# Four chained attention blocks on one core: row fills copied by VectorE, positions moved, and the DMAs of the transposed maxima issued by GpSimd

## The chip, the cores and the metric

The kernel runs on one core of a Trainium2 chip. A core has TensorE (PE: matmuls and transposes, results in PSUM), VectorE (DVE), ScalarE (ACT), GpSimd (POOL) and SyncE (SP). SP only issues DMAs here; DMAs can also be issued by ACT and POOL. The engines run side by side, each through its own program in order, and wait for each other by semaphores. The metric is the device time of one execution in microseconds (us); lower is better.

## The reference

Sixteen batches of 128 tokens with 128 channels go through four blocks. `ctx` is a second input of the same shape.

```python
# L0: 8 heads of 16
h = layernorm(x);  c = layernorm(ctx)
x = x + softmax(q(h) @ k(c).T / 4) @ v(c)
# L1: 16 heads of 8, causal and key padding mask, query padding
x = x + where(query_ok, softmax(where(mask, q(x) @ k(ctx).T / 8**.5, -inf)), 0) @ v(ctx)
# L2: 16 heads, then a gelu network of width 512
x = x + attn(x, ctx) @ Wo + bo;  x = x + gelu_tanh(x @ W1 + b1) @ W2 + b2
# L3: self attention (causal, padding), cross attention, gelu network; a layernorm behind each
x = ln(x + selfattn(x) @ Wo1 + bo1)
x = ln(x + crossattn(x, ctx) @ Wo2 + bo2)
x = ln(x + gelu(x @ W1 + bf1) @ W2 + bf2)
```

All is float32. The maximum of each row of scores is taken off before the exponential.

## The kernel before

Two batches make a pair; eight pairs go through five parts (L0, L1, L2, L3S for the self attention, L3C for the cross attention and the rest), which gives 40 **units**, numbered u = 8 * part + pair. A unit is 128 partitions by 256 tokens, and its two batches are b = 0 and 1. Within a batch heads go in groups of four (two groups in L0, four in the others).

Scores are computed in bfloat16 with float32 accuracy. Queries and keys are split into three bfloat16 terms (ACT makes the first in "split"; POOL the others in "rest", "term1" and "term2", lines 525, 527 and 533), and six DMAs ("stack", line 432) lay products of terms row above row in a tile `pairs`, so that one matmul of 52 (L0: 96) rows gives the scores of one head. Under these rows lie four mask rows (parts L1 and up) and three rows that carry the negated row maximum.

Each group of scores is computed twice. First "score" (line 861): the result goes to DVE, which takes the maximum of each row (`max_words`, line 754). When a batch's groups are done DVE makes three terms of the maxima ("nmax", lines 764 and 767), PE transposes them ("n_tr", line 926), DVE copies the result to `max_rows` (line 770), and a DMA of 6 or 12 KB (line 448) puts them into the three rows of `pairs`. Then "attn" (line 947) computes the transposed scores with the maximum already taken off, ACT takes the exponential (`probs`, line 651), and "pv" (line 974) multiplies by the values. The first attn group of a batch waits for that batch's DMA of maxima (semaphore `max_landed`). From L1 on each attn group is interleaved with the score group of the next unit with the same b and number.

The order of all work is a table written out by hand. Every step has a position relative to eight times its unit's number (`PREPARE`, `STACK_AT`, `SCORE_AT`, `CHAIN` and so on), `schedule()` sorts the steps, and each engine runs its share of this one list in that order. A unit thus takes eight positions; its preparation begins up to 41 positions before its own attention, and the chain behind it ("a_tr", "wo", "x_tr", "w1", "w2", "out", "store") ends up to 47 positions after. The list sets no time: an engine that waits for one step holds all steps behind it.

Four engines matter for the change. SP issues, in list order, the loads of tokens (line 367), the six stack DMAs of each unit, the mask rows (line 424), the weights (line 395) and the DMAs of maxima (line 448), each behind a semaphore wait. Before the first stack DMA it issues four DMAs (line 380) that write the mask rows' query side and rows of ones for L1 to L3 into `pairs16`; their source is `constant_rows`. POOL computes the terms, the layer norms' reciprocal roots (`var_eps` and `rstd`, lines 517 and 520), the squares of the gelu (line 538), the mask rows and the last scaling (lines 545 and 549). DVE also does the layer norm's statistics and normalisation in L0 (`stats`, `normed_in`, lines 688 to 707). ACT issues four small DMAs of ones for L0 (line 558).

## Time and profile before

| | |
|---|---|
| median of three runs | 515.94 us (515.82 to 528.79) |
| the profiled execution | 511.9 us, its span 510.2 us |
| busy over the span | PE 89%, DVE 77%, ACT 64%, POOL 42% |
| mean granted TensorE clock | 0.948 of full speed |
| chain of waits, by engine | PE 64%, DVE 15%, DMA 7%, ACT 4%, SP's queue 4%, POOL 2% |
| maxima in the chain of waits (line 448's DMAs) | 5.4% of the span |

The span is the profiled part of one execution; the execution's own time is 1.7 us more. Busy shares are means over stages that differ: L0 runs from 34.6 us (the first attn group) to about 109 us, L1 to 191, L2 to 285, L3S to 382, L3C to the end, of which the last 33 us hold no attention any more but the chains of the last three units. A busy PE is not PE at its peak, since matmul ends are modelled.

### The profile page before, as it was taken

How to read it: one execution, taken by the hardware profiler on the slowest of the kernel's cores; microseconds unless marked ns; L12 is line 12 of the kernel's file. 1: busy time of each engine (PE TensorE's matmuls, PEld its weight loads, DVE VectorE, ACT ScalarE, POOL GpSimd, SP SyncE). 2: the span in 40 equal slices, each digit the busy share in tenths (PEclk: the TensorE clock that was granted, in tenths of full speed). 3: DMA queues.
4: the chain of work that ended last, by engine and by line, in shares of the span. 5: the costliest groups of instructions: out<-in, count | busy, mean ns of one | idle time of the engine just before them, and what ended most of it. 6: DMA issues, size and time to landing. Idle time of an engine off the chain costs nothing.

```text
span 510.2 us, 17171 instructions
## 1 busy us (share of the span) xinstructions
PE 455.2 (89%) x6720; PEld 306.4 (60%) x6720; DVE 391.7 (77%) x1093; ACT 325.2 (64%) x660; POOL 216.4 (42%) x256
## 2 busy tenths in 40 slices
PE   3578998799998897999999999999999899998873
PEld 2466666466665565666666666666666556665552
DVE  6669887488787776789887777888889977886362
ACT  2436666347765676677777677576777687777541
POOL 3745388465442234244444344333436434222153
PEclk9667899799999998899999999999999999999798
DMA  5634444445454443232232322223343322200000
GB/s 130 142 88 108 120 104 100 90 108 137 111 121 101 100 94 89 65 81 74 64 75 63 69 66 64 67 66 71 73 91 88 86 66 65 46 14 26 10 16 26
DMA packets 72750, 40.45 MB, mean 79 GB/s; under 512 B 7100, under 2 KB 71900, under 8 KB 72672
## 3 DMA queue, kind: packets, MB, share of 16 engines
q1 hardware_dynamic: 72564, 39.26, 33.0%
q8 instruction: 55, 0.90, 0.7%
q14 instruction: 23, 0.19, 0.1%
q10 hardware_dynamic: 108, 0.10, 0.1%
HBM read 4.74 MB, written 1.05 MB: 11 GB/s over the span
## 4 chain that ended last, share of the span: by engine, by line
PE 64%; DVE 15%; DMA 7%; ACT 4%; issue 4%; SPq 4%; POOL 2%; POOLq 0%; DVEq 0%; ACTq 0%
PE attn_ps L947 13%; PE o_ps L974 12%; PE misc_ps L1004 6%; DMA pairs<-max_rows 5%; DVE max_words L754 5%; PE misc_ps L995 4%; PE misc_ps L981 4%; PE misc_ps L909 4%; PE score_ps L828 3%; PE misc_ps L910 3%; DVE normed_in L707 3%; PE misc_ps L915 2%; SPq L432 2%; PE misc_ps L987 2%; PE misc_ps L926 2%
## 5 line engine op out<-in xcount | busy, mean ns | idle before, releaser
L754 DVE TENSOR_REDUCE max_words<-score_ps 128x4 f32<-128x512 f32 x288 | 194.6, 683 | 50.8 <-PE score_ps L861 47.5
L651 ACT ACTIVATE probs<-attn_ps 128x512 f32<-128x512 f32 x288 | 169.5, 599 | 86.9 <-PE attn_ps L947 80.3
L947 PE MATMUL attn_ps<-pairs 55*128 55x128 bf16 (+1 forms) x1152 | 115.5, 223 | 18.4 <-DMA pairs<-max_rows 10.6
L861 PE MATMUL score_ps<-pairs 52*128 52x128 bf16 (+1 forms) x1152 | 115.4, 223 | 0.5 <-DMA pairs<-terms 0.4
L525 POOL TENSOR_TENSOR rest<-qk_f,terms 128x512 f32<-128x512 f32 x40 | 46.5, 1162 | 147.1 <-ACT terms L602 147.1
L947 PEld LDWEIGHTS attn_ps<-pairs 55*128 55x128 bf16 (+1 forms) x1152 | 66.0, 96 | 63.6 <-issue 28.9
L974 PE MATMUL o_ps<-probs,v 128*32 128x128 f32 x2304 | 98.8, 285 | 0.1
L861 PEld LDWEIGHTS score_ps<-pairs 52*128 52x128 bf16 (+1 forms) x1152 | 68.6, 97 | 3.5 <-DMA pairs<-terms 1.0
L974 PEld LDWEIGHTS o_ps<-probs,v 128*32 128x32 f32 x2304 | 54.3, 110 | 23.6 <-issue 10.6
L533 POOL TENSOR_TENSOR terms<-rest,terms 128x512 bf16<-128x512 f32 x40 | 46.3, 1158 | 14.6 <-DVE max_words L767 12.2
L527 POOL TENSOR_TENSOR terms<-qk_f,terms 128x512 bf16<-128x512 f32 x40 | 46.3, 1158 | 0.0
L660 ACT ACTIVATE o_sb<-o_ps 128x256 f32<-128x256 f32 x80 | 30.8, 385 | 23.2 <-PE o_ps L974 22.8
L517 POOL TENSOR_SCALAR var_eps<-mean_var 128x2 f32<-128x2 f32 (+1 forms) x32 | 7.1, 223 | 79.6 <-DVE mean_var L692 79.4
L981 PE MATMUL misc_ps<-ident,o_sb 128*128 128x128 f32 x160 | 35.7, 306 | 0.1
L1004 PE MATMUL misc_ps<-hidden,w 128*128 128x256 f32 x128 | 33.6, 399 | 2.4 <-ACT hidden L639 2.4
L796 DVE SCALAR_TENSOR_TENSOR xT<-misc_ps,col,xT 128x256 f32<-128x256 f32 x40 | 19.2, 482 | 19.6 <-PE misc_ps L1004 14.0
L995 PE MATMUL misc_ps<-xT,w 128*128 128x256 f32 x128 | 30.9, 384 | 0.1
L1004 PEld LDWEIGHTS misc_ps<-hidden,w 128*128 128x128 f32 x128 | 23.5, 194 | 8.1 <-ACT hidden L639 2.8
L538 POOL TENSOR_TENSOR gelu_arg<-half_h 128x512 f32<-128x512 f32 x16 | 16.3, 1039 | 27.9 <-ACT half_h L636 27.9
L520 POOL TENSOR_TENSOR rstd<-var_eps,minus_half 128x2 f32<-128x2 f32 (+1 forms) x32 | 25.4, 794 | 2.7
L590 ACT ACTIVATE qk_f<-misc_ps,col 128x256 f32<-128x256 f32 x24 | 11.4, 474 | 22.7 <-PE misc_ps L910 21.3
L602 ACT ACTIVATE terms<-qk_f 128x512 bf16<-128x512 f32 x40 | 25.1, 629 | 0.6
(108 smaller groups left out, 741.7 us busy)
## 6 DMA issues: line engine op xcount, KB each, us to landing
pairs<-terms SPq DMA_DIRECT2D x240, 128.0 KB
w<-in_weights_dram SPq DMA_DIRECT2D x5, 320.0 KB, 4.8
x_tok<-in_x_dram SPq DMA_DIRECT2D x8, 128.0 KB, 2.4
c_tok<-in_ctx_dram SPq DMA_DIRECT2D x8, 128.0 KB, 2.5
pairs<-max_rows SPq DMA_DIRECT2D x64, 12.0 KB
out_dram<-x_tok SPq DMA_DIRECT2D x8, 128.0 KB, 1.8
w<-in_weights_dram SPq DMA_DIRECT2D x3, 192.0 KB, 2.5
pairs<-constant_rows SPq DMA_DIRECT2D x4, 112.0 KB
```

The costliest lines, as they stand in the source:

```text
L525: pool.tensor_tensor(rest[:, :, :], qk_f32[:, :, :], terms[:, :, 0, :], ALU.subtract)
L527: pool.tensor_tensor(terms[:, :, 1, :], qk_f32[:, :, :], terms[:, :, 0, :], ALU.subtract)\
L533: pool.tensor_tensor(terms[:, :, 2, :], rest[:, :, :], terms[:, :, 1, :], ALU.subtract)\
L651: act.activation(probs[n % PROBS_RING][:, :, :].rearrange("p h q -> p (h q)"), attn_ps[n % 2][:, :], ACT.Exp, scale=float(D // HEADS[part] ...
L660: act.activation(o_sb[n % 2][:, :], o_ps[:, 0:2 * P], ACT.Copy)\
L754: dve.tensor_reduce(max_words[ub(step) % 2][:, QUAD * g:QUAD * (g + 1)], score_ps[n % 2][:, :].rearrange("p (h k) -> p h k", h=QUAD), AX_X ...
L861: return pe.matmul(score_ps[NUM[step] % 2][:, j * S:(j + 1) * S], tile[score_rows(u), QUAD * g + j, 0, b * S:(b + 1) * S], tile[score_rows ...
L947: last = pe.matmul(attn_ps[n % 2][:, j * S:(j + 1) * S], pairs[attn_rows(u), h, 1, b * S:(b + 1) * S], pairs[attn_rows(u), h, 0, b * S:(b ...
L974: last = pe.matmul(o_ps[32 * j:32 * j + 32, region * P:(region + 1) * P], values, probs[n % PROBS_RING][:, j, :], start=part == L0 or g % ...
L981: last = pe.transpose(bank[:, k * P:(k + 1) * P], o_sb[ub(step) % 2][:, k * P:(k + 1) * P], ident[:, :])
L995: last = pe.matmul(bank[:, half * TOK:(half + 1) * TOK], weight(f"w1_{part}_{2 * b + half}"), xT[s][:, :], start=True, stop=True)
L1004: last = pe.matmul(bank[:, 0:TOK], weight(f"w2_{part}_{c}"), hidden[:, c, :], start=(c == 0), stop=(c == 3))
```

## The change

Seven things change.

1. The four DMAs of `constant_rows` into `pairs16` go. POOL builds a `template` of 128 partitions and DVE copies its rows, 32 partitions by 4096 float32 words, four times (`fill_rows`, line 384). Two copies stand behind the first `ln_norm`, one each behind the second and third. DVE's two zero fills of `v16` move to the end of L0's preparation.
2. All token loads are issued first, before any stack DMA.
3. The mask rows of L1's first four units are issued at four steps of L0's later units, not with the stack DMAs.
4. Weights come in smaller pieces in the order of use, and L2, L3S and L3C each wait for their own.
5. Every DMA of maxima is issued by POOL, at the same step "n_tr" of the list as before by SP. POOL first waits for DVE's copy.
6. Many positions move. Units 0 and 2 are prepared three and one positions earlier (`LAG`).
7. The chains of units 36 to 39 have positions of their own (`LAST`), which interleave them.

```diff
--- before.py
+++ after.py
-W_NAMES = ([f"{m}{p}" for p in range(PARTS) for m in "qkv"] + ["o2", "o3", "o4"]
-           + [f"w1_{l}_{c}" for l in (2, 4) for c in range(4)] + [f"w2_{l}_{c}" for l in (2, 4) for c in range(4)])
+W_NAMES = ([f"{m}{p}" for p in (0, 1) for m in "qkv"]
+           + [f"{m}2" for m in "qkvo"] + [f"{m}_2_{c}" for m in ("w1", "w2") for c in range(4)]
+           + [f"{m}{p}" for p in (3, 4) for m in "qkvo"] + [f"{m}_4_{c}" for m in ("w1", "w2") for c in range(4)])
 W_AT = {n: i for i, n in enumerate(W_NAMES)}
 W_FIRST = 3
-W_SECOND = 6
-W_SOME = 5
-W_PIECES = -(-(len(W_NAMES) - W_SECOND) // W_SOME)
+W_SECOND, W_THIRD, W_FOURTH = W_AT["q2"], W_AT["q3"], W_AT["q4"]
+W_EACH = {L1: 3, L2: 2}
+W_PIECES = {L2: (W_THIRD - W_SECOND) // W_EACH[L1], L3S: (W_FOURTH - W_THIRD) // W_EACH[L2],
+            L3C: (len(W_NAMES) - W_FOURTH) // W_EACH[L2]}
...
 PREPARE = {
-    L0: (("load", -41), ("ln_in", -34), ("raw_tr", -29), ("ln_norm", -31), ("ln_tr", -26),
-          ("qk", -24), ("split", -23), ("rest", -18), ("term1", -18), ("term2", -18), ("v", -20),
-          ("mask", 24)),
+    L0: (("ln_in", -34), ("raw_tr", -29), ("ln_norm", -31), ("ln_tr", -26), ("qk", -24),
+          ("split", -23), ("rest", -20), ("term1", -18), ("term2", -18), ("v", -19), ("mask", 24)),
     L1: (("qk", -26), ("split", -25), ("rest", -22), ("term1", -20), ("term2", -18), ("v", -13)),
-    L2: (("qk", -26), ("split", -25), ("rest", -24), ("term1", -21), ("term2", -21), ("v", -13)),
-    L3S: (("qk", -26), ("split", -25), ("rest", -23), ("term1", -21), ("term2", -21), ("v", -14)),
-    L3C: (("qk", -26), ("split", -25), ("rest", -25), ("term1", -25), ("term2", -21), ("v", -13)),
+    L2: (("qk", -27), ("split", -25), ("rest", -25), ("term1", -25), ("term2", -24), ("v", -15)),
+    L3S: (("qk", -26), ("split", -25), ("rest", -25), ("term1", -22), ("term2", -21), ("v", -14)),
+    L3C: (("qk", -26), ("split", -25), ("rest", -25), ("term1", -22), ("term2", -22), ("v", -13)),
 }
-STACK_AT = {L0: -17, L1: -19, L2: -22, L3S: -22, L3C: -22}
+STACK_AT = {L0: -17, L1: -19, L2: -20, L3S: -24, L3C: -18}
...
+LAG = {0: -3, 2: -1}
+LAST = {
+    36: (("a_tr", 13), ("wo", 15), ("x_tr", 19), ("x_stats", 21), ("x_norm", 23), ("x_back", 26),
+          ("w1", 27), ("w1", 27), ("w2_first", 29), ("w2", 29), ("x_tr", 34), ("x_stats", 38),
+          ("x_norm", 43), ("out", 43), ("store", 47)),
...
+            put(pos + LAG.get(u, 0), Step(kind, u, 0, 0))
...
+        for kind, pos in LAST.get(u, CHAIN[part]):
...
+        def fill_rows(dve, r):
+
+            if r == 0:
+                dve.wait_ge(rows_ready, 5)
+            rows_ = slice(HALF * (r % 2) + QUARTER, HALF * (r % 2 + 1))
+            dve.tensor_copy(pairs16[r // 2][rows_, :, :, :].rearrange("p h a n -> p h (a n)").bitcast(F32),
+                            template[rows_, :, :, :].rearrange("p a b n -> p (a b n)").bitcast(F32).unsqueeze(1)
+                            .to_broadcast([HALF - QUARTER, 16, TOK])).then_inc(fill16_done, 1)
+
...
+            for s in range(SETS):
+                first = s * PAIR
+                sp.dma_start(x_tok[s][:, :, :], x[first:first + PAIR].rearrange("b t d -> t b d"))\
+                    .then_inc(tokens_landed[s], 16)
+                sp.dma_start(c_tok[s][:, :, :], ctx_in[first:first + PAIR].rearrange("b t d -> t b d"))\
+                    .then_inc(tokens_landed[s], 16)
+                if s == 0:
...
-                if step.kind == "load" and u == 2:
-
-                    sp.wait_ge(rows_ready, 4)
-                    for r in range(RING):
-                        tile, base = pairs16[r // 2], HALF * (r % 2) + product_rows(SETS)
-                        sp.dma_start(tile[base:base + MASK_ROWS + TERMS, :, :, :].rearrange("p h a n -> p h (a n)"),
-                                     constant_rows[:, :, :, :].rearrange("p a b n -> p (a b n)").unsqueeze(1)
-                                     .to_broadcast([MASK_ROWS + TERMS, 16, 2 * TOK])).then_inc(fill16_landed, 16)
...
+                if step == the("attn", u) and part == L0 and u >= RING:
+
+                    r = u % RING
+                    sp.wait_ge(fill16_done, r + 1)
+                    sp.wait_ge(mask_l1_ready, r + 1)
+                    mask_rows(sp, SETS + r)
...
-                if step.kind == "n_tr":
-
-                    evacuated(sp, step)
-                    n = ub(step)
-                    if n == 0:
-                        sp.wait_ge(fill8_landed, 16 * RING)
-                    tile, base = stack_of(u)
-                    last_row = attn_rows(u).stop
-                    sp.dma_start(tile[last_row - TERMS:last_row, :, 0, step.b * S:(step.b + 1) * S],
-                                 max_rows[n % 4][0:TERMS * heads, :]).then_inc(max_landed[n % 4], 16)
...
+            pool.memset(template[:, :, :, :], 1.0).then_inc(ones_ready, 1)
...
+                if step.kind == "n_tr":
+
+                    evacuated(pool, step)
+                    n = ub(step)
+                    if n == 0:
+                        pool.wait_ge(fill8_landed, 16 * RING)
+                    tile, base = stack_of(u)
+                    last_row = attn_rows(u).stop
+                    pool.dma_start(tile[last_row - TERMS:last_row, :, 0, step.b * S:(step.b + 1) * S],
+                                 max_rows[n % 4][0:TERMS * HEADS[u // SETS], :]).then_inc(max_landed[n % 4], 16)
...
                 if kind == "ln_norm" and u == 0:
-
-                    for ring in range(RING // 2, RING):
-                        dve.memset(v16[ring][:, :, :], 0.0).then_inc(v_zeroed, 1)
+                    fill_rows(dve, 0)
+                    fill_rows(dve, 1)
+                if kind == "ln_norm" and u == 1:
+                    fill_rows(dve, 2)
+                if kind == "ln_norm" and u == 2:
+                    fill_rows(dve, 3)
+                if kind == "ln_norm" and u >= SETS - 2:
+
+                    ring = u % RING
+                    dve.memset(v16[ring][:, :, :], 0.0).then_inc(v_zeroed, 1)
...
-                    if u == L2 * SETS:
-                        pe.wait_ge(weights_landed, 16 * W_PIECES)
+                    if part >= L2 and s == 0:
+                        pe.wait_ge(weights_landed[part], 16 * W_PIECES[part])
```

On DVE at the start of its program the four copies stand where the two zero fills (MEMSET of v_2 and v_3) stood. Before, from the first unit's normalisation on:

```order
10 L707 TENSOR_SCALAR normed_in<-x_tok,mean_var,rstd 128x128 x2
11 L707 TENSOR_SCALAR normed_in<-c_tok,mean_var,rstd 128x128 x2
12 L714 MEMSET v_2 128x1056
13 L714 MEMSET v_3 128x1056
...
18 L698 TENSOR_SCALAR half_m<-col 128x4
19 L688 BN_STATS stats<-x_tok 128x6 x2
```

The same place in the changed kernel:

```order
11 L749 TENSOR_SCALAR normed_in<-c_tok,mean_var,rstd 128x128 x2
12 L384 COPY pairs_0<-template 32x4096 x2
13 L740 TENSOR_SCALAR half_m<-col 128x4
14 L730 BN_STATS stats<-x_tok 128x6 x2
...
18 L749 TENSOR_SCALAR normed_in<-c_tok,mean_var,rstd 128x128 x2
19 L384 COPY pairs_1<-template 32x4096
20 L798 TENSOR_TENSOR v_0<-misc_ps,row 128x8x16 x2
```

Two copies now stand ahead of the second unit's statistics, and one behind its normalisation (the fourth stands behind the third unit's).

On POOL in L2, before: the three operations that make a unit's terms, then the two squares of the gelu.

```order
130 L525 TENSOR_TENSOR rest<-qk_f,terms 128x512
131 L527 TENSOR_TENSOR terms<-qk_f,terms 128x2x256
132 L533 TENSOR_TENSOR terms<-rest,terms 128x2x256
133 L538 TENSOR_TENSOR gelu_arg<-half_h 128x512 x2
```

And in the changed kernel:

```order
165 L557 TENSOR_TENSOR rest<-qk_f,terms 128x512
166 L559 TENSOR_TENSOR terms<-qk_f,terms 128x2x256
167 L565 TENSOR_TENSOR terms<-rest,terms 128x2x256
168 L575 DMA pairs_1<-max_rows 3x16x128
169 L580 TENSOR_TENSOR gelu_arg<-half_h 128x512 x2
170 L575 DMA pairs_0<-max_rows 3x16x128
```

Each of a unit's two DMAs of maxima stands behind work of other units on POOL.

On PE at the very end, before, from the network's second product of unit 37 on (L1004 is "w2", L1010 "x_tr", L995 "w1", L1016 "x_back"):

```order
2912 L1004 MATMUL misc_ps<-hidden,w 128x256 x2
2913 L1016 MATMUL misc_ps<-ident,normed 128x128 x2
2914 L1010 MATMUL misc_ps<-ident,xT 128x128 x4
2915 L995 MATMUL misc_ps<-xT,w 128x256 x4
2916 L1004 MATMUL misc_ps<-hidden,w 128x256 x4
2917 L1016 MATMUL misc_ps<-ident,normed 128x128 x2
2918 L1010 MATMUL misc_ps<-ident,xT 128x128 x2
2919 L995 MATMUL misc_ps<-xT,w 128x256 x4
```

And in the changed kernel, where the same steps are L1054, L1060, L1045 and L1066:

```order
2919 L1054 MATMUL misc_ps<-hidden,w 128x256 x2
2920 L1060 MATMUL misc_ps<-ident,xT 128x128 x2
2921 L1045 MATMUL misc_ps<-xT,w 128x256 x4
2922 L1060 MATMUL misc_ps<-ident,xT 128x128 x2
2923 L1054 MATMUL misc_ps<-hidden,w 128x256 x2
2924 L1066 MATMUL misc_ps<-ident,normed 128x128 x2
2925 L1054 MATMUL misc_ps<-hidden,w 128x256 x2
2926 L1045 MATMUL misc_ps<-xT,w 128x256 x4
```

A transpose of another unit now stands between "w1" and "w2" of a unit, and "w1" of unit 39 directly behind "w2" of unit 38.

## Rows read from the trace of the kernel before

**Rows 1.** Busy time by stretch: length, each engine's busy us (instructions), clock, DMA share, GB/s.

```profile
34.50:109.20 74.70, 66.42 (x712) 45.87 (x714) 57.91 (x176) 41.12 (x90) 43.12 (x50) 0.87 0.45 108
109.20:190.80 81.60, 77.32 (x1620) 49.62 (x1616) 63.99 (x172) 54.08 (x105) 33.51 (x35) 1.00 0.48 109
...
285.40:382.30 96.90, 96.40 (x1716) 63.16 (x1714) 77.69 (x207) 66.85 (x133) 37.15 (x40) 1.00 0.31 71
...
477.00:510.20 33.20, 21.72 (x125) 16.00 (x124) 13.69 (x49) 10.49 (x24) 11.44 (x20) 0.86 0.06 16
```

**Rows 2.** Who waited for whom: us in total, times, longest.

```profile
PE attn_ps L947 <- DMA pairs<-max_rows: 10.6, 7, 3.5
...
PE attn_ps L828 <- DMA pairs<-max_rows: 1.9, 4, 1.4
...
PE misc_ps L909 <- DMA w<-in_weights_dram: 1.4, 1, 1.4
```

**Rows 3.** Chain of waits: start, us, from issue to landing.

```profile
32.54 1.98 DMA pairs<-max_rows
...
88.97 4.75 DMA pairs<-max_rows
...
130.44 3.48 DMA pairs<-max_rows
```

**Rows 4.** Issues of the DMA of maxima on SP: ns least, median, most.

```profile
L448 SPq DMA_DIRECT2D pairs<-max_rows x80: 698/757/782, 32.5 to 467.4; - x80
```

**Rows 5.** Groups by shape: count, busy us, mean ns, idle before, releaser.

```profile
L668 DVE MEMSET v<- 128x1056 f32 x2 | 1.9, 938 | 0.3 <-issue 0.3
...
L525 POOL TENSOR_TENSOR rest<-qk_f,terms 128x512 f32<-128x512 f32 x40 | 46.5, 1162 | 147.1 <-ACT terms L602 147.1
...
L520 POOL TENSOR_TENSOR rstd<-var_eps,minus_half 128x4 f32<-128x4 f32 x8 | 8.3, 1040 | 0.7
...
L479 POOL TENSOR_SCALAR mask_rows_l<-valid_raw 4x256 bf16<-4x256 uint8 x8 | 8.5, 1061 | 0.7
```

**Rows 6.** Timeline of the start, DVE and POOL: start, us.

```profile
19.13 1.55 DVE L707 TENSOR_SCALAR normed_in<-x_tok,mean_var,rstd 128x128 f32<-128x128 f32 x2 [3.13 <-POOL rstd L520]
20.60 2.42 DVE L707 TENSOR_SCALAR normed_in<-c_tok,mean_var,rstd 128x128 f32<-128x128 f32 x2
...
19.45 1.15 POOL L525 TENSOR_TENSOR rest<-qk_f,terms 128x512 f32<-128x512 f32 x1 [0.35 <-ACT terms L602]
```

**Rows 7.** Timeline: copies of maxima and the attn groups that need them.

```profile
69.62 0.20 DVE L770 COPY max_rows<-misc_ps 24x128 bf16<-24x128 bf16 x1
...
72.40 0.40 PE L947 MATMUL attn_ps<-pairs 99*128 99x128 bf16 x4
...
220.81 0.20 DVE L770 COPY max_rows<-misc_ps 48x128 bf16<-48x128 bf16 x1
...
223.69 0.23 PE L947 MATMUL attn_ps<-pairs 55*128 55x128 bf16 x1
```

**Rows 8.** Timeline in L2 around one copy of maxima.

```profile
215.32 0.20 DVE L770 COPY max_rows<-misc_ps 48x128 bf16<-48x128 bf16 x1
...
216.21 1.16 POOL L533 TENSOR_TENSOR terms<-rest,terms 128x512 bf16<-128x512 f32 x1
...
218.83 0.23 PE L947 MATMUL attn_ps<-pairs 55*128 55x128 bf16 x1
```

**Rows 9.** Timeline of PE at the end, its waits in brackets.

```profile
474.86 0.60 PE L947 MATMUL attn_ps<-pairs 55*128 55x128 bf16 x4 [2.06 <-ACT probs L651]
...
494.23 1.97 PE L1004 MATMUL misc_ps<-hidden,w 128*128 128x256 f32 x8 [1.02 <-ACT hidden L639]
...
496.87 0.41 PE L1010 MATMUL misc_ps<-ident,xT 128*128 128x128 f32 x2 [0.45 <-DVE xT L796]
...
500.30 1.97 PE L1004 MATMUL misc_ps<-hidden,w 128*128 128x256 f32 x8 [1.02 <-ACT hidden L639]
...
502.94 0.41 PE L1010 MATMUL misc_ps<-ident,xT 128*128 128x128 f32 x2 [0.67 <-DVE xT L796]
```

More of the change, by code:

```diff
@@ L89 @@
 PV_TURN = {L0: 0, L1: 1, L2: 1, L3S: 1, L3C: 1}
-O_TR_AFTER = {L0: 3, L1: 2, L2: 2, L3S: 2, L3C: 2}
+O_TR_AFTER = {L0: 4, L1: 2, L2: 3, L3S: 2, L3C: 2}
 CHAIN = {
@@ L132, in schedule @@
         for kind, pos in PREPARE[part]:
-            put(pos, Step(kind, u, 0, 0))
+            put(pos + LAG.get(u, 0), Step(kind, u, 0, 0))
         for c in range(len(PRODUCTS)):
-            put(STACK_AT[part] + (c // 2 if part == L0 else c), Step("stack", u, c, 0))
+            put(STACK_AT[part] + LAG.get(u, 0) + (c // 2 if part == L0 else c), Step("stack", u, c, 0))
         for b in range(PAIR):
@@ L147, in schedule @@
         seen = {}
-        for kind, pos in CHAIN[part]:
+        for kind, pos in LAST.get(u, CHAIN[part]):
             seen[kind] = seen.get(kind, -1) + 1
@@ L264, in build @@
         first_landed = sem("first_landed")
-        weights_landed = sem("weights_landed")
+        weights_landed = {part: sem(f"weights_landed{part}") for part in (L2, L3S, L3C)}
         second_landed = sem("second_landed")
@@ L360, in _ @@
         def _(sp):
+            for s in range(SETS):
[5 more added lines that the diff above has]
+                if s == 0:
+                    sp.dma_start(w[:, 0:W_FIRST, :], weights[:, 0:W_FIRST, :]).then_inc(first_landed, 16)
+                    sp.dma_start(col[:, :], cols).then_inc(first_landed, 16)
+                    sp.dma_start(row[:, :, :], rows.partition_broadcast(P)).then_inc(first_landed, 16)
             for step in STEPS:
@@ L387, in _ @@
                     sp.dma_start(pad_raw[:, :], pad.partition_broadcast(P)).then_inc(masks_landed, 16)
-                if step.kind == "load" and u == SETS - 1:
+                if step.kind == "ln_in" and u == 5:
                     sp.dma_start(w[:, W_FIRST:W_SECOND, :], weights[:, W_FIRST:W_SECOND, :])\
                         .then_inc(second_landed, 16)
-                if step.kind == "v" and 0 <= u - SETS - 1 < W_PIECES:
-                    first = W_SECOND + (u - SETS - 1) * W_SOME
-                    some = slice(first, min(first + W_SOME, len(W_NAMES)))
-                    sp.dma_start(w[:, some, :], weights[:, some, :]).then_inc(weights_landed, 16)
+                if step.kind == "v" and part in W_EACH:
+                    from_, to = (W_SECOND, W_THIRD) if part == L1 else (W_THIRD, len(W_NAMES))
+                    first = from_ + (u % SETS) * W_EACH[part]
+                    some = slice(first, min(first + W_EACH[part], to))
+                    if first < to:
+                        user = L2 if first < W_THIRD else L3S if first < W_FOURTH else L3C
+                        sp.dma_start(w[:, some, :], weights[:, some, :]).then_inc(weights_landed[user], 16)
+                if step == the("attn", u) and part == L0 and u >= RING:
[3 more added lines that the diff above has]
+                    mask_rows(sp, SETS + r)
                 if step.kind == "stack":
```

91 lines of the change are left out of this document (50 added, 41 removed).

## The prediction, made before the changed kernel ran

> **What bounds the kernel now.** I read the busy time by stretch first [rows 1]. TensorE is busy 96.4 of 96.9 us in L3S at the full clock, so nothing that only frees another engine can shorten that stretch, and whatever makes TensorE wait there is paid in full. The idle time that a change can win lies elsewhere: 74.7 - 66.4 = 8.3 us in L0, 81.6 - 77.3 = 4.3 us in L1, and 33.2 - 21.7 = 11.5 us behind the last attention. In L0 TensorE is not alone: GpSimd is busy 43.1 of 74.7 us there. The list of waits says what ends the idle time in L0 to L2: TensorE waits 10.6 + 1.9 = 12.5 us for DMAs of maxima and 1.4 us for weights [rows 2]. The chain of waits shows why the DMAs are late. One on an empty queue lands 1.98 us after its issue begins, one in L1, behind the stack DMAs, takes 3.48 us, and the one at 88.97 us, behind mask rows and stack DMAs, 4.75 us [rows 3]. Issuing one holds SP for 0.76 us [rows 4].
>
> The quantity that decides is the lead: the time from VectorE's copy of the maxima to the moment at which TensorE could start the attn group that needs them. I paired all 80 copies with their groups in the timeline and took off what TensorE waited for the DMA. In L0 most leads are 1.8 to 3.1 us, as 72.40 - 69.62 = 2.78; in L1 3.2 to 3.9; in L2 2.9 for the first batch of a unit, as 223.69 - 220.81 = 2.88, and 3.5 or more for the second; in L3 3.0 to 6.5 [rows 7]. A DMA that lands later than its lead makes TensorE wait for the difference.
>
> **The sum** starts at the profiled execution, 511.9 us; the median of the runs shown is 4.0 us above it, and I add that at the end.
>
> *The copies of rows.* VectorE loses two zero fills here (of the shape of the first two, 1.9 us together [rows 5]) and gets four copies of 4096 words per partition. No row shows a large copy. A zero fill of 1056 words takes 0.938 us [rows 5], which scales to 3.6 us; at twice that rate it is 1.8 us. These are my bounds, and I take 2.5, a little below the middle, since a plain copy is the simplest operation that VectorE has and the fill's rate includes its fixed part. Two copies stand ahead of the second unit's statistics and push back its `rstd`, and since GpSimd works in order, also the first unit's "rest" behind it. One can hide in the 3.13 us that VectorE waited for `rstd` before 19.13 us [rows 6]. The first attention group moves by 4 x 2.5 - 1.9 - 3.1 = **+5.0** us (with the bounds +2.2 to +9.4). In the same rows the four normalisations beside GpSimd's "rest" take from 19.13 to 23.02, so large VectorE and GpSimd operations in SBUF do not overlap freely, and a copy will not hide under "rest".
>
> *The DMAs of maxima leave SP.* The 12.5 us of waits go: **-12.5**. In their place stand those of a DMA issued by GpSimd, which no row of this trace shows. I call L the time from the start of the copy to the landing. Its lower bound is 1.98 plus 0.2 for the copy, 2.2 us; the upper one is what a loaded queue gives, 3.48 + 0.2 = 3.7 us. GpSimd has a queue of its own, so the stack DMAs need not be drained first, but it makes the transfer in software: its operations cost 1.0 to 1.2 us where SP's issue costs 0.76 [rows 4, 5]. I take the middle, 2.9 us. Adding up L minus lead wherever that is positive over the 80 pairs gives 2.3 us for L = 2.2, **+7.1** for L = 2.9 (5.7 in L0, 1.4 in L2), and 26.8 for L = 3.7. That slope is the largest uncertainty here.
>
> The Trainium skill, "DMA: Bandwidth & Descriptors", Specifications, gives about 1 us to the first byte for a DMA issued by GpSimd and about 0.6 us for one by SP; by that difference L would be an estimated 2.6 us and this term 4.3 instead of 7.1.
>
> *GpSimd in order.* The DMA now also waits for what stands ahead of it on GpSimd. In L2 "rest", "term1" and "term2" do. In the trace "term2" of such a unit ends at 216.21 + 1.16 = 217.37, while the copy came at 215.32 and the attn group at 218.83 [rows 8]. Issued at 217.4, the DMA lands 2.65 us later, at 220.0: 1.2 us late. The order has this pattern for units 17 to 20; the last has lead enough. Three times 1.2, and 0.4 for first batches that wait for the end of the two squares, is **+4** us (0 to 8). In L0 GpSimd's work per unit is 3 x 1.16 + 1.06 + 1.04 = 5.6 us [rows 5] and some 0.6 of small operations; with two DMAs of about 1 us it becomes 8.2, where the units from 72.40 us to the stall that ended at 93.72 took (93.72 - 3.5 - 72.40) / 2.5 = 7.1 us each [rows 2, 3, 7]. I take 1.1 for each of three such units, **+3** us (0 to 8). In the other direction "rest" now waits behind a DMA that waits for its copy; the stack DMAs have six or more positions to spare, so this costs nothing; if that cover went, the score groups would wait.
>
> *SP.* It no longer waits for copies of maxima, so its stack DMAs and mask rows leave when their terms are ready. Only TensorE's wait for weights, **-1.4** [rows 2], is worth something: each part now waits for its own pieces. The earlier token loads are 16 short issues done before the first terms exist, and the 4 DMAs of rows that go away were hidden behind the start's computation: nothing.
>
> *The end.* TensorE waits 2.06 + 1.02 + 0.45 + 1.02 + 0.67 = 5.2 us in five places [rows 9]. "w2" of unit 36 now stands where TensorE waited for the exponential, and transposes of other units between "w1" and "w2". The wait for the gelu of unit 39 and the last transpose stay in part. I take **-4.5** us (0 to -6). Behind the last matmul nothing changes. The other moved positions lie in stretches in which TensorE is full, and I cost them at nothing.
>
> 511.9 + 5.0 - 12.5 + 7.1 + 4 + 3 - 1.4 - 4.5 = 512.6, and with the 4.0 of the median **516.6 us**: what is won in waits is given back by the path through GpSimd and by the start. A change under about 2% (10.3 us) can hardly be told from none here.
>
> **The rivals.**
>
> *Faster: the own queue is all gain.* GpSimd issues as quickly as SP, L is 2.2 (-4.8), the copies run at 1.8 us (-2.8), and of the 7 us of holding only 2 remain (-5): 504.0 us. For it speaks that the least landing, 1.98 us, came on an empty queue, and GpSimd's always is. Against it speaks that GpSimd is the slowest engine per operation in this trace.
>
> *Slower: the software path takes the place of the backlog.* If a DMA through GpSimd needs L = 3.7, the term is 26.8 instead of 7.1: 536.3 us. The place is every unit of L0 and the first batches of L2, where leads are 2.8 to 2.9 us. The case turns slower than 2% at L of about 3.3 us, where 10 us have been added. It needs only 0.4 us more than I assume. Against it: 80 such DMAs are small, and in L3 the leads are long.
>
> *Slower: VectorE locks GpSimd out.* Each unit of L0 has four normalisations, which took 1.55 us for two beside GpSimd [rows 6]. If one DMA in each of the eight units is held for that long, it adds 12.4: 529.0 us. The Trainium skill, "SBUF — State Buffer", has this as a trap in its section on two separate sides: an fp32 copy on VectorE keeps GpSimd from writing descriptors. The trace agrees that the two engines hinder each other, but only with GpSimd's arithmetic; it has no DMA of GpSimd's to show.
>
> *The end does not do what it says.* Each chain there is a string of dependent steps over four engines, and a new order may only move the waits: +4.5, 521.1 us.
>
> **How the numbers follow.** My case has a chance of 0.30, the end without gain 0.10, the faster rival 0.28, the software path 0.26, the lock 0.06. Faster by over 2% (under 505.6 us): 0.28. Within 2%: 0.30 + 0.10 = 0.40. Slower (over 526.3): 0.26 + 0.06 = 0.32. With the other terms at their bounds (start -2.8 to +4.4, holding -5 to +9, the two taken one at a time) my own case reaches from 511 to 526. The range for 8 in 10 takes in most of both rivals: 500 to 537 us.
>
> **What would show it.** Copies of 2 to 3 us on VectorE and the first attn group at 39 to 40 us, not 34.6, confirm the first term. The time from the copy of maxima to the attn groups that wait for it gives L directly: 2.9 confirms the second, 2.2 or 3.7 a rival. TensorE's wait for DMAs of maxima should be some 14 us in all, now in L0 and L2 and gone from L1. GpSimd's issues in L2 should begin at the end of "term2". The stretch behind the last attn group should be 29 to 31 us long. The prediction is wrong if issuing takes GpSimd well over 1.2 us, or if the moved positions change the long TensorE-bound stretches, which I took as fixed.

## The result, and the profile after

| | before | changed |
|---|---|---|
| median | 515.88 us (four runs, 513.78 to 528.79) | 584.73 us (four runs, 582.93 to 587.08) |
| ratio to before, 95% interval | | 1.1353 [1.1284, 1.1422] |
| profiled execution, span | 511.9, 510.2 us | 586.13, 584.4 us |
| granted TensorE clock, mean | 0.948 | 0.882 |

The change costs 69 us, far outside the range of 500 to 537. A median here is over all executions of a kernel, while a ratio compares only those in the chip's usual state, at its fuller clock, and is left out where they were too few. The busy times by stretch of the changed kernel answer to [rows 1]; here they cover L0, L1, L2, L3S, L3C and the stretch behind the last attention (length, busy us of PE, PEld, DVE, ACT, POOL with their instructions, clock, DMA share, GB/s).

```profile
37.90:131.60 93.70, 79.03 (x710) 51.61 (x710) 67.99 (x188) 42.14 (x90) 51.90 (x65) 0.72 0.34 82
131.60:232.30 100.70, 88.43 (x1622) 54.63 (x1619) 65.92 (x170) 51.95 (x104) 44.89 (x52) 0.88 0.38 80
232.30:350.70 118.40, 99.76 (x1298) 67.95 (x1300) 84.71 (x194) 69.47 (x145) 51.86 (x53) 0.87 0.29 63
350.70:453.40 102.70, 96.42 (x1706) 62.92 (x1703) 82.51 (x207) 65.53 (x131) 48.48 (x56) 0.98 0.31 67
453.40:557.00 103.60, 90.08 (x1205) 60.93 (x1205) 76.06 (x216) 71.99 (x142) 40.97 (x58) 0.97 0.21 46
557.00:584.40 27.40, 17.06 (x116) 12.76 (x114) 13.55 (x54) 10.15 (x24) 13.81 (x24) 0.92 0.09 25
```

Against before, L0 is 19.0 us longer, L1 19.1, L2 23.8 (it was 94.6), L3S 5.8, L3C 8.9 (it was 94.7), and the last stretch 5.8 shorter. TensorE executes the same 6720 matmuls, yet is busy 487.8 us instead of 455.2: in L0 and L1 it is 12.6 and 11.1 us busier, at a clock of 0.72 and 0.88 of full speed where it was 0.87 and 1.00. So of the 74.2 us by which the span grew 32.6 are longer busy time of the same matmuls, more of which ran at the lower of the two clocks (1.2 GHz), and 41.6 us are idle time. The list of waits of the changed kernel (who waited for whom: us, times, longest) answers to [rows 2]:

```profile
PE attn_ps L997 <- DMA pairs<-max_rows: 19.4, 11, 3.9
PE attn_ps L997 <- issue: 16.7, 6, 4.1
PE attn_ps L878 <- DMA pairs<-max_rows: 13.5, 9, 2.7
```

The "issue" row belongs to the DMAs too. Its six waits are the second batches of units 16 to 20 and of unit 33: that of unit 17 ended at 254.60, when the DMA copied at 249.11 and issued only at 251.01 had landed, 3.5 us after its issue. TensorE thus waits 49.6 us for maxima, not the 12.5 of before. The row of the issuing line (ns least, median, most, and its landings) answers to [rows 4]:

```profile
L575 POOL DMA_DIRECT2D pairs<-max_rows x80: 562/613/789, 35.9 to 548.8; - x80
...
DMA to landing us min/median/max: 1.7/2.6/7.0
```

Issuing takes GpSimd 0.61 us, less than SP's 0.76. But the landing comes anywhere from 1.7 to 7.0 us later. The mean of all 80 is 3.13 us. From the copy's start to the issue it is 0.50 us at the least and 0.68 in the mean (0.23 on SP), so L, from the copy's start to the landing, is 3.8 us in the mean (3.3 in L0, 4.3 in L1, 3.8 in L2 and in L3), or 3.6 without what GpSimd holds.

What sets the landing is seen in the timeline of SP and GpSimd around a slow one (start, us, engine, line, what; idle before in brackets; SPq is SP's queue of instructions):

```profile
142.38 3.27 SPq L468 DMA_DIRECT2D pairs<-terms  x5
145.68 0.47 SPq L433 DMA_DIRECT2D w<-in_weights_dram  x1
...
146.24 0.61 POOL L575 DMA_DIRECT2D pairs<-max_rows  x1 [2.65 <-DVE max_rows L820]
...
146.26 0.70 SPq L396 DMA_DIRECT2D pairs<-mask_rows_l  x1
```

Five stack DMAs of 128 KB and one of weights were issued in the 3.9 us ahead of it. It landed after 5.4 us, and TensorE waited 2.7 of them. The number of DMAs ahead does not say it all: up to unit 5, landings behind four to six DMAs of SP still took 1.8 to 3.6 us. In L3 most landings whose burst reached to within 1 us of the issue take 4 to 7 us, and most of those with a quiet SP ahead 2.1 to 2.5. In the kernel before this burst came 0.8 us *behind* each DMA of maxima: SP, waiting for the copy, held it back, and it had mostly drained 5 us later when the next one was due.

The other engine that changed is VectorE, busy 422.0 us instead of 391.7; 10.1 are the row copies. The timeline of POOL and DVE at one "nmax" of L0:

```profile
44.79 0.56 POOL L575 DMA_DIRECT2D pairs<-max_rows  x1 [3.37 <-DVE max_rows L820]
45.37 1.18 POOL L557 TENSOR_TENSOR rest<-qk_f,terms 128x512 f32<-128x512 f32 x1
46.48 1.17 POOL L559 TENSOR_TENSOR terms<-qk_f,terms 128x512 bf16<-128x512 f32 x1
...
45.33 2.35 DVE L814 TENSOR_TENSOR max_words<-max_words 128x8 f32<-128x8 f32 x1
```

An operation on 8 words per partition takes 2.35 us and ends with GpSimd's second subtraction. By shape, the groups that this stretches most (before: 262 and 726 ns):

```profile
L814 DVE TENSOR_TENSOR max_words<-max_words 128x8 f32<-128x8 f32 x16 | 15.8, 988 | 0.5
L859 DVE SCALAR_TENSOR_TENSOR hidden<-gelu_arg,half_h 128x512 f32<-128x512 f32 x16 | 18.9, 1218 | 0.0
```

The Trainium skill, "SBUF — State Buffer", section "Who interferes with whom", says that a VectorE instruction with two inputs in SBUF contends with a GpSimd instruction that reads SBUF, and that whichever issues first holds the shared ports for its whole instruction while the other stands. The trace agrees in part: the 2.35 us end when GpSimd is through, but VectorE stands through two of its instructions, although its own record begins 0.04 us ahead of the first.

### The profile page after: what moved, and what is told of

Same layout as the page of the kernel before. It is cut to its first block, busy times and chain, and to the rows that moved or that the text cites. A ratio compares the mean times of both kernels' runs of the same rounds, so it can differ in the third digit from the quotient of the medians.

```text
span 584.4 us, 17180 instructions
## 1 busy us (share of the span) xinstructions
PE 487.8 (83%) x6720; PEld 323.6 (55%) x6720; DVE 422.0 (72%) x1097; ACT 323.3 (55%) x660; POOL 272.3 (47%) x337
## 4 chain that ended last, share of the span: by engine, by line
PE 48%; DVE 20%; DMA 16%; issue 7%; POOL 7%; ACT 2%; POOLq 0%; DVEq 0%; ACTq 0%
DMA pairs<-max_rows 16%; PE attn_ps L997 11%; PE o_ps L1024 9%; DVE max_words L804 6%; PE misc_ps L1054 5%; PE misc_ps L959 4%; PE misc_ps L1045 3%; DVE hidden L859 3%; DVE max_words L814 3%; PE misc_ps L960 3%; PE score_ps L911 2%; PE score_ps L878 2%; PE misc_ps L1031 2%; POOL terms L559 2%; PE misc_ps L976 2%
## 5 line engine op out<-in xcount | busy, mean ns | idle before, releaser
L997 PE MATMUL attn_ps<-pairs 55*128 55x128 bf16 (+1 forms) x1152 | 121.9, 232 | 39.3 <-DMA pairs<-max_rows 19.4
L575 POOL DMA_DIRECT2D pairs<-max_rows x80 | 50.0, 625 | 185.8 <-DVE max_rows L820 181.5
L911 PE MATMUL score_ps<-pairs 52*128 52x128 bf16 (+1 forms) x1152 | 123.1, 233 | 0.9 <-DVE max_words L804 0.9
L997 PEld LDWEIGHTS attn_ps<-pairs 55*128 55x128 bf16 (+1 forms) x1152 | 69.5, 99 | 88.3 <-issue 53.8
L1024 PE MATMUL o_ps<-probs,v 128*32 128x128 f32 x2304 | 105.1, 299 | 0.2 <-issue 0.2
L911 PEld LDWEIGHTS score_ps<-pairs 52*128 52x128 bf16 (+1 forms) x1152 | 72.2, 101 | 5.1 <-issue 1.6
L1024 PEld LDWEIGHTS o_ps<-probs,v 128*32 128x32 f32 x2304 | 56.8, 115 | 27.2 <-issue 15.0
L559 POOL TENSOR_TENSOR terms<-qk_f,terms 128x512 bf16<-128x512 f32 x40 | 49.3, 1234 | 0.6
L814 DVE TENSOR_TENSOR max_words<-max_words 128x16 f32<-128x16 f32 (+1 forms) x80 | 32.8, 410 | 2.7
L1054 PE MATMUL misc_ps<-hidden,w 128*128 128x256 f32 x128 | 33.3, 388 | 1.7 <-ACT hidden L681 1.6
L632 ACT ACTIVATE qk_f<-misc_ps,col 128x256 f32<-128x256 f32 x24 | 11.4, 474 | 39.6 <-PE misc_ps L960 21.2
L1045 PE MATMUL misc_ps<-xT,w 128*128 128x256 f32 x128 | 32.6, 399 | 0.3 <-DVE xT L862 0.3
L846 DVE SCALAR_TENSOR_TENSOR xT<-misc_ps,col,xT 128x256 f32<-128x256 f32 x40 | 19.0, 479 | 11.1 <-PE misc_ps L1054 6.6
L959 PE MATMUL misc_ps<-xT,w 128*128 128x256 f32 x64 | 26.5, 502 | 0.0
L1054 PEld LDWEIGHTS misc_ps<-hidden,w 128*128 128x128 f32 x128 | 22.9, 190 | 6.4 <-ACT hidden L681 2.0
```

The lines of the kernel that those rows point to most:

```text
L559: pool.tensor_tensor(terms[:, :, 1, :], qk_f32[:, :, :], terms[:, :, 0, :], ALU.subtract)\
L575: pool.dma_start(tile[last_row - TERMS:last_row, :, 0, step.b * S:(step.b + 1) * S], max_rows[n % 4][0:TERMS * HEADS[u // SETS], :]).then_ ...
L814: dve.tensor_tensor(second, first, upper_half(words, 0, heads), ALU.subtract)\
L911: return pe.matmul(score_ps[NUM[step] % 2][:, j * S:(j + 1) * S], tile[score_rows(u), QUAD * g + j, 0, b * S:(b + 1) * S], tile[score_rows ...
L959: pe.matmul(bank[:, 0:TOK], weight(f"q{part}"), qsrc[:, :], start=True, stop=True)
L997: last = pe.matmul(attn_ps[n % 2][:, j * S:(j + 1) * S], pairs[attn_rows(u), h, 1, b * S:(b + 1) * S], pairs[attn_rows(u), h, 0, b * S:(b ...
```

## The experiments

Each was timed in three rounds beside the kernel before on the same chip. "SP's version" is the first of them.

**Who issues.** SP again, in the changed kernel; GpSimd, in the kernel before and nothing else; ScalarE, in the changed kernel. (The code shown in this part is shortened; a comment says where a line stands.)

```diff
-                if step.kind == "n_tr":          # in the GpSimd block
-                    evacuated(pool, step)
...
+                if step.kind == "n_tr":          # in the SP block, as before
+                    evacuated(sp, step)
...
```

> The changed kernel, but the DMAs of the maxima are issued by SP again, where the kernel before has them; VectorE's row copies, the split weights and all moved positions stay. Theory A (lost gate): once SP no longer waits for a copy of maxima, it issues its stack DMAs ahead of the maxima's DMA, which then lands 4 to 5.5 us after its issue instead of about 2; putting it back on SP restores the order, so the waits of TensorE for maxima fall from 49.6 us to about 10 and the time to 505 to 518 us. Theory B (slow path: GpSimd's queue is slower by itself): the same time. Theory C (the moved positions cost the time): it stays above 560 us.

> The kernel before with this one edit: the DMAs of the maxima are issued by GpSimd from its own queue, at the same place of the order. Theories A and B: most of the 69 us comes with this edit alone, 560 to 590 us. Theory C: within 2% of the kernel before, about 520 us.

> The changed kernel, but ScalarE issues the DMAs of the maxima from its own hardware queue; SP waits for nothing, as in the changed kernel. Theory A: SP still runs ahead, so landings stay at 4 us or more where stack DMAs are under way, and the time is 560 to 590 us. Theory B: a hardware queue lands in about 2 us, TensorE's waits fall to 10 to 15 us, and the time is 510 to 525 us, with some 0.7 us of ScalarE's time per DMA (54 us in all) that its idle time hides.

| | median us | ratio to before |
|---|---|---|
| SP issues | 504.05 | 0.9728 [0.9665, 0.9790] |
| the same, timed again | 510.64 | 0.9866 [0.9768, 0.9963] |
| before, GpSimd issues | 578.78 | 1.1208 [1.1123, 1.1293] |
| ScalarE issues | 540.94 | 1.0439 [1.0363, 1.0515] |

The second row is a repetition, made later as the base of other runs:

> The version in which SP issues the maxima, once more, as the base of the two before it on this chip: 502 to 507 us by every theory.

The issuing engine is the whole loss and more: without it the change is 1.3 to 2.7% faster, and alone in the kernel before it costs 12.1%. The moved positions are not to blame (theory C falls). The repetition came out at 510.6 us where 502 to 507 was expected, so this base is known to some 1%. ScalarE lies in between, so neither theory A alone nor B alone will do. TensorE's waits for maxima in SP's version:

```profile
PE attn_ps L997 <- DMA pairs<-max_rows: 5.7, 7, 1.7
...
PE attn_ps L878 <- DMA pairs<-max_rows: 2.1, 2, 1.8
```

**The order of the queues.** GpSimd issues; SP gets a wait back at the place where it issued the maxima. Three kinds, one in each kernel: for the landing, for VectorE's copy, and for GpSimd's having issued (for this GpSimd writes one word behind its DMA and raises a semaphore with it).

```diff
+                if step.kind == "n_tr":          # in the SP block
+                    sp.wait_ge(max_landed[n % 4], (n // 4 + 1) * 16)   # for the landing
+                    evacuated(sp, step)                                # for the copy
+                    sp.wait_ge(issued, ub(step) + 1)                   # for the issue
```

> The changed kernel, with GpSimd still issuing the DMAs of the maxima, and one wait added: at the place where SP issued such a DMA, it now waits until that DMA has landed, so none of its later stack DMAs can be ahead of it. Theory A: the landings of 4 to 5.5 us fall to 1.8 to 2.4 us after the issue, TensorE's waits for them to 10 to 15 us, the granted clock comes back, and the time is 515 to 530 us. Theory B: landings stay above 4 us in L1, and the time stays within 2% of 585 us or gets worse, since the stack DMAs are only later.

> The changed kernel, GpSimd issuing, and SP waits, where it issued a DMA of maxima before, only for VectorE's copy of the maxima. Its burst of six stack DMAs then starts at the copy, 0.3 us ahead of GpSimd's DMA, and is over well before the next copy; with the wait for the landing (the gate tried before) it started 2 us later and ran into the next maxima. Theory A (burst ahead in the DMA engines): landings above 4 us disappear, TensorE's waits for maxima fall from 49.6 to 15 to 25 us, the time is 520 to 545 us. Theory B (the software path and GpSimd itself are slow, whatever stands in the queues): landings keep their spread and the time stays at 565 to 590 us.

> The changed kernel, GpSimd issuing, and SP waits where it issued a DMA of maxima before until GpSimd has issued its own (GpSimd raises a semaphore with a write of one word behind the DMA). The burst of stack DMAs now starts behind the maxima's DMA, as when SP issued both. Theory A (what stands ahead in the DMA engines sets the landing): landings of 2.1 to 2.5 us nearly everywhere, instead of the 3.1 us mean of the gate on the copy; waits for maxima fall from 33 to about 15 us; 525 to 545 us. Theory B (the software path's own slowness): landings stay near 3.1 us and the time at 555 to 570 us. What then remains above SP's 504 us is copy to issue on GpSimd, 0.50 and more against 0.23 us, and VectorE held while GpSimd works.

| SP waits for | median us | ratio to before | issue to landing, least / median / most | mean |
|---|---|---|---|---|
| nothing (changed kernel) | 584.73 | 1.1353 | 1.7 / 2.6 / 7.0 | 3.13 |
| the landing | 572.04 | 1.1042 [1.0954, 1.1130] | 1.8 / 2.7 / 5.4 | 3.02 |
| the copy | 562.40 | none (four executions: 555.56, 558.09, 566.70, 572.33) | 2.1 / 3.2 / 4.5 | 3.11 |
| the issue | 547.51 | 1.0663 [1.0555, 1.0770] | 1.7 / 2.1 / 4.7 | 2.28 |

The two lowest executions of the wait for the copy give about 1.08, an estimate. All three expectations of theory A were too low in time (the last by 2.5 us), but the landings follow the order of the queues each time. Waiting for the landing moved the burst of each step to just ahead of the *next* DMA. Waiting for the copy put one stack DMA 0.2 to 0.3 us ahead of nearly every DMA of maxima and the others behind it; only three landings took 4 us or more, but few took 2. Waiting for the issue put all of it 0.7 us behind, as SP alone does. The same DMA as above (unit 9, second batch) in that kernel:

```profile
141.44 0.61 POOL L579 DMA_DIRECT2D pairs<-max_rows  x1 [4.70 <-DVE max_rows L825]
142.04 0.09 POOL L581 MEMSET told<- 1x1 f32 x1
...
142.16 1.94 SPq L470 DMA_DIRECT2D pairs<-terms  x3
```

The row of its landing:

```profile
DMA to landing us min/median/max: 2.1/2.1/2.1
```

It is 2.1 us instead of 5.4. The order is worth 1.1353 - 1.0663 = 0.069 of the time before, 36 us (29 to 42 by the two intervals). It does not explain what is left: the wait for the issue is still 0.080 to 0.094 above SP's version, 41 to 48 us. The same wait for the copy, added to the kernel in which ScalarE issues:

> The kernel in which ScalarE issues the DMAs of maxima (540.9 us), with the same wait for the copy put back on SP. Theory A: only the missing gate cost it anything against SP's issue (504 us), so it comes to 503 to 515 us. Theory B: what it costs is that ScalarE waits for the copy and issues, so the time stays at 535 to 545 us.

533.06 us, 1.0370 [1.0293, 1.0447], against 1.0439 without the wait: the intervals overlap, so no gain is shown. Theory A's 503 to 515 is missed, and B is the nearer one. That ScalarE pays mostly for waiting and issuing in its own order would fit, but is not shown: on GpSimd the wait for the copy left one stack DMA ahead, and the wait for the issue was not tried with ScalarE.

**What GpSimd's DMAs do to others.** SP issues the maxima, GpSimd 80 DMAs of the same size that nobody needs (only GpSimd itself waits for each, four of them later); then only its waits for the copies; then only the DMAs.

```diff
+                if step.kind == "n_tr":          # in the GpSimd block of SP's version
+                    evacuated(pool, step)        # left out in the third
+                    pool.dma_start(spare[n % 4][0:rows_, :], ident_bf[0:rows_, :])\
+                        .then_inc(spare_landed[n % 4], 16)                          # and this in the second
```

> The version in which SP issues the maxima (504 us), and GpSimd issues 80 more DMAs of the same size at the same steps, from the identity into a spare tile, for which nobody waits. It tells the latency of GpSimd's DMAs from what they do to others. If GpSimd's time, its waiting for the copies and the hold on VectorE cost most of the loss: 530 us or more, with the two-input operation on the maxima of L0 near 1 us on VectorE instead of 0.33. If the latency for TensorE is what costs: 504 to 512 us.

> The version in which SP issues the maxima (504 us); GpSimd only waits for VectorE's copy at each of these steps and issues nothing. Theory H (hold): the 33.7 us of the idle DMAs come from this wait, since 'rest', 'term1' and 'term2' behind it now start at the copy and run beside VectorE's two-input operations: 525 to 540 us, hidden<-gelu_arg near 1.2 us on VectorE instead of 0.70. Theory D (the DMAs' own work): 504 to 510 us and 0.70.

> The same version; GpSimd issues the 80 idle DMAs at these steps without waiting for the copies. Theory H: 504 to 512 us, as GpSimd has 50 us more of work and is idle half the time. Theory D: 530 us or more, since issuing holds VectorE.

| GpSimd does | median us | ratio to before | VectorE: `hidden`, `max_words` of 8, ns |
|---|---|---|---|
| nothing more | 504.05 and 510.64 | 0.9728 and 0.9866 | 702, 326 |
| wait and DMA | 537.74 | 1.0516 [1.0344, 1.0688] | 1331, 1136 |
| wait only | 507.83 | 0.9832 [0.9757, 0.9908] | 1096, 463 |
| DMA only | 522.47 | no interval (514.36 to 528.83) | 702, 506 |

DMAs for which nobody waits cost 0.065 to 0.079 of the time before, 34 to 41 us. But 4.6 us of that come after all computation: GpSimd's closing drain ends late, in both kernels with idle DMAs. The drain with the DMAs alone, and in the repetition of SP's version (ns, then the us at which it begins):

```profile
L216 POOLq DRAIN  x1: 7376/7376/7376, 512.3 to 512.3; - x1
...
L216 POOLq DRAIN  x1: 829/829/829, 508.1 to 508.1; - x1
```

In the changed kernel, where the DMAs are waited for, the drain takes 2.16 us and holds nothing up, so the price that bears on it is 29 to 36 us, some two fifths of the gap to SP's version. Neither theory H nor D holds alone. The wait alone costs nothing that shows, although it stretches `hidden` to 1096 ns; the DMAs alone cost some 12 us by the medians against the base timed beside them, 4.6 of them this drain; together the two seem to cost more than the sum, though the intervals are wide. The wait ties GpSimd's subtractions to the copy, and the DMA ahead of them puts them off by 0.55 us, into VectorE's next "nmax". VectorE and its effect on TensorE in the kernel that does both:

```profile
L869 DVE SCALAR_TENSOR_TENSOR hidden<-gelu_arg,half_h 128x512 f32<-128x512 f32 x16 | 20.7, 1331 | 0.0
L824 DVE TENSOR_TENSOR max_words<-max_words 128x8 f32<-128x8 f32 x16 | 18.2, 1136 | 0.5
```

```profile
PE misc_ps L1047 <- DVE attn_tok L850: 8.4, 6, 2.0
PE misc_ps L986 <- DVE max_words L827: 6.6, 11, 1.4
PE attn_ps L1007 <- DVE max_words L814: 4.1, 6, 1.1
PE attn_ps L1007 <- DMA pairs<-max_rows: 4.0, 4, 1.2
```

TensorE now waits for VectorE, and hardly for maxima: all its waits for VectorE are 39.5 us, against 25.1 in the repetition of SP's version. With the drain's 4.6 that is 19 of the 22.0 us between the two spans (533.1 and 511.1). That the subtractions' new place is the reason is my reading of these rows, and no run moved the subtractions alone. The kernel in which SP waits for the issue is slower than SP's version in another way: of 35.5 us of span (546.6) 20.4 are longer busy time of TensorE at a lower clock, 6.5 more waiting for VectorE and 5.3 more for maxima. So the price of the idle DMAs cannot be carried over to it, or to the changed kernel (27.6 us of waits for VectorE), as one and the same item.

**The price of a delay.** SP issues one more DMA, of one row, between the copy and the DMA of maxima: in SP's version, and in the kernel before.

```diff
+                    sp.dma_start(spare[n % 4][0:1, :], ident_bf[0:1, :]).then_inc(spare_landed[n % 4], 16)
                     sp.dma_start(tile[last_row - TERMS:last_row, :, 0, step.b * S:(step.b + 1) * S],
```

> The version in which SP issues the maxima, with one more DMA of one row, for which nobody waits, issued by SP between the copy and the maxima's DMA. It makes the landing later by one issue on SP, 0.6 to 0.7 us, and changes nothing else. By my sum over the leads (2.3 us for L = 2.2, 7.1 for L = 2.9) it costs about 5 us: 507 to 512. If the leads react to a delay, each landing putting off the next copy, and the clock falls with the waits, it costs 15 to 35 us: 519 to 539.

> The kernel before with one more DMA of one row issued by SP between the copy and the maxima's DMA, so that each lands one issue of 0.65 us later. My sum over the leads of this kernel gives 5 us from L = 2.2 to 2.9 and 20 from 2.9 to 3.7; with landings between these, 4 to 13 us: 520 to 530. If delays feed on each other, as in the version with the moved positions (14 us), more than 13: 531 or more.

518.16 us, 1.0086 [1.0026, 1.0146], in the first: 11 to 19 us above SP's version by the ratios. In the kernel before 526.33 us, 1.0214 [1.0136, 1.0292]: 7 to 15 us. In the kernel before that is some 17 us per us of delay, and within the 4 to 13 us that my sum gave for it (7 per us between L = 2.2 and 2.9, 25 per us beyond): delays feeding on each other, 531 us or more, did not show. With the moved positions the sum gave 5 us, and the cost is two to four times that. Waits for maxima in the kernel before with the delay were

```profile
PE attn_ps L953 <- DMA pairs<-max_rows: 19.3, 13, 3.7
...
PE attn_ps L834 <- DMA pairs<-max_rows: 6.2, 7, 1.9
```

which is 25.5 us instead of 12.5, while the time grew by 11: some of the new waits took the place of other ones.

**Rows and positions.** SP's version with the positions of before; the kernel before with the moved positions; and the latter with the split weights as well. (SP issues the maxima in all three.)

> The changed kernel with SP issuing the maxima and all step positions of the kernel before; what is left of the change are VectorE's row copies, the split of the weights, the token loads at the start and the earlier mask rows. By my terms: +5.0 for the copies and -1.4 for the weights, 519 to 522 us against a kernel before of 517. If the positions are not what made SP's version fast, it is 503 to 508 us.

> The kernel before with the moved positions alone (the tables, LAG and LAST); SP issues the maxima, constant rows come by DMA, weights as before. By my terms: -4.5 at the end and nothing elsewhere, 511 to 514 us. If the positions are what made SP's version fast (504 us against 517.4), it is 498 to 506 us, with waits of TensorE for maxima in L0 to L2 below the 12.5 us of before.

> The kernel before with the moved positions and the split weights; SP issues the maxima and the constant rows come by DMA. Positions alone gave 506.3 us with TensorE waiting 2.2 us for weights; without that wait 503 to 505 us, as fast as or faster than the version with VectorE's row copies (504).

| | median us | ratio to before |
|---|---|---|
| rows, weights, loads; old positions | 525.88 | 1.0228 [1.0144, 1.0312] |
| moved positions alone | 506.32 | 0.9852 [0.9795, 0.9910] |
| moved positions and split weights | 501.11 | 0.9742 [0.9583, 0.9901] |

The positions are the gain. On the old table the rest of the change costs 2.3%, 12 us, three times my 3.6; on the new one the same rest costs nothing that shows. With the positions alone L2 takes 90.5 us instead of 94.5, L3S 94.5 instead of 96.9, and L3C with all that follows 119.0 instead of 127.9, while L0 and L1 together take 165.4 instead of 156.2. The waits for maxima hardly change (12.2 us, 12.5 before). With positions and weights and no row copies the kernel is the fastest of all medians, 2.6% under before; against SP's version of the full change the difference is not told apart.

## Why the prediction was wrong

In the terms of the sum, TensorE's waits for maxima were put at 7.1 + 4 + 3 = 14.1 us and came to 49.6, and its busy time was put at no change and grew by 32.6. Together these are 68 us, as much as the forecast missed by; what the other terms missed nearly cancels.

*The step that failed* is the one on SP: "It no longer waits for copies of maxima, so its stack DMAs and mask rows leave when their terms are ready", of which I said that only the wait for weights is worth something. That wait was the gate that kept six large DMAs behind a small urgent one. I had even the rows for it, since the landings of [rows 3] grow from 1.98 to 4.75 us with what stands ahead. But I took this for a matter of the queue ("GpSimd has a queue of its own, so the stack DMAs need not be drained first"). A separate queue does not help: the small DMA still stands behind them, with the same 2.1 against 5.4 us. Price: 36 us of the 68.

*L* was forecast at 2.9 us and measured at 3.6 without what GpSimd holds, where my rival "the software path" stood (3.7). Its reason was another one: with the order put back, the landing takes 2.1 us at the median, against 1.98 for SP's on an empty queue (the profile has SP's landings only where they stand in the chain of waits). As far as these rows show, the software path itself adds only the 0.27 us from copy to issue and what GpSimd holds.

*The clock* was left out of the sum. L0 to L2 need 33.1 us more of busy TensorE, at 0.72, 0.88 and 0.87 of the full clock. Most of it came with the issuing engine: in SP's version TensorE is busy 457.3 us, 30.5 less. But why the clock fell is open. In L2 it goes with the waits (1.00 in SP's version). In L1 it does not: SP's version is at 0.90 there with 4.1 us idle, the kernel before at 1.00 with 4.3, and the kernel before with the later issue still at 1.00 with 8.3. The rival of the software path, at 536.3 us, missed by 48 us for the uneven landings (1.7 to 7.0 us around their mean), for the clock and for what follows.

*GpSimd in order.* The place was right: the long holds of L2 are there (copy to issue 2.15, 1.90, 1.51 and 1.56 us in the second batches of units 16 to 19, against 0.50 in most others). The size was not, 4 us: the waits behind them are 4.1, 4.0, 2.4 and 2.8 us, for the landing behind the burst comes on top. The longest hold of all is in L0: the second batch of unit 3 was issued 3.58 us after its copy, behind "term1", "term2" and a `rstd`, and TensorE waited 2.6 us. And I counted only what GpSimd makes its own DMAs wait for. What it does to VectorE when its arithmetic moves I had costed at nothing; together with the rest of what idle DMAs do it is 29 to 36 us in the kernel that has them.

*VectorE locks GpSimd out* named the right pair of engines in the wrong direction. In the 80 issues GpSimd takes 0.56 to 0.79 us and never stands for 1.5. It is VectorE that stands, behind GpSimd's subtractions. The trap that the Trainium skill, "SBUF — State Buffer", section "SBUF: two separate sides", has for VectorE's fp32 copies and descriptors written by GpSimd does not show in these issues; the four copies of rows could not show it, since the last begins at 26.1 us and GpSimd's first DMA at 35.95.

*Right were* the copies of rows (three take 2.28 us and one 3.24; 2.5 forecast), the first attn group (37.9 us; 39.6 forecast) and the removal of the waits for weights. *The end* was right in its number, by luck in part: it takes 27.4 us instead of 33.2, so -5.8 against -4.5. But 4.7 of these are busy time (116 matmuls instead of 125, at a clock of 0.92 instead of 0.86), and the idle time, from which the forecast took all of its gain, fell by 1.1 only. *The stretches in which TensorE is full* were not fixed, in either direction: L3S is 102.7 us with late maxima, and 94.5 in SP's version against 96.9 before. The moved positions alone bring 1.5%, more than the 4.5 us (0.9%) that I gave the end, although they lengthen L0 and L1.

In shares of the time before: SP's version -0.013 to -0.027, GpSimd's idle DMAs +0.065 to +0.079 (0.009 of it the closing drain), from these to maxima issued by GpSimd in order +0.015 (1.0663 - 1.0516; +0.024 without the drain, with some 0.02 to either side), the lost order +0.069. These are differences between neighbouring kernels and add up to +0.135 by construction. The issuing engine and the order are shown by runs that change them alone; how the rest divides between VectorE, latency and clock stays open.

## What to carry to other kernels

A semaphore wait on a busy DMA issuer may be doing useful work: it keeps bulk transfers behind an urgent small one. Before moving the urgent DMA to another queue, list what the old issuer will send early once it no longer waits, and, if it moves, give the old issuer a wait for the *issue* of the urgent one (not for its landing, nor for its data). Here even the best of these stayed 6.6% slower than leaving the DMA where it was. And when GpSimd gets new work in the middle of its order, look at which two-input operations of VectorE its arithmetic will now run beside. An experiment with work that nobody waits for needs a look at the end of its trace, too: such work may be paid for in the closing drain.

## What the runs showed of the hardware that was not expected

- A DMA of 12 KB on a queue of its own (GpSimd's) landed 2.1 to 2.5 us after its issue in most cases with SP quiet ahead of it, and in L1 and L3 mostly 4 to 7 us after it behind five or more DMAs, most of 128 KB, that SP had issued within 4 us. Where these came 0.7 us later than it, the median of all was 2.1 us.
- The issue itself took GpSimd 0.61 us (0.56 to 0.79) and SP 0.76; but it began 0.50 us after the start of VectorE's copy on GpSimd and 0.23 us after it on SP.
- A VectorE operation of two inputs with 8 words per partition took up to 2.41 us beside GpSimd's subtractions, and 0.17 at the least.
- With 80 DMAs on GpSimd's queue for which no other engine waited, GpSimd's closing drain took 7.38 us; with 80 for which TensorE waited, 2.16; with none, 0.83. What makes the difference was not tried.
